# A Mamba scan on one core: weighted states added in pairs on VectorE, their sums transposed by TensorE, states ordered in pairs

## The reference

```
xb, z = split(x @ in_w.T)
xb = silu(causal_conv(xb, 4 taps) + cb)
delta, Bm, Cm = split(xb @ xp_w.T, [16, 16, 16])
delta = softplus(delta @ dtw.T + dtb)
dA = exp(delta[..., None] * -exp(a_log))
mi = delta[..., None] * Bm[:, :, None, :] * xb[..., None]
v = 0.6 * v + mi_t
h = dA_t * h + v
y_t = einsum("ben,bn->be", h, C_t)
y = (y + dp * xb) * silu(z)
out = y @ ow.T
```

## Time and profile before

| | us |
|---|---|
| median of 3 runs | 2259.93 (2258.51 to 2260.69) |
| profiled execution | 2258.78 |
| its span on the core | 2257.5 |
| TensorE busy | 1946.5 (86%) |
| TensorE weight loads | 1554.8 (69%) |
| VectorE busy | 1383.8 (61%) |
| GpSimd busy | 991.2 (44%) |
| ScalarE busy | 913.2 (40%) |

### The profile page before, as it was taken

The page is one execution under the profiler, slowest core; times in us unless marked ns, Lnnn a source line. Parts: engine busy times, 40 slices in busy tenths (PEclk is TensorE's granted clock), DMA queues, the critical chain, the costliest instruction groups (busy, mean ns, idle before and its releaser), DMA issues.

```text
span 2257.5 us, 31075 instructions
## 1 busy us (share of the span) xinstructions
PE 1946.5 (86%) x12488; PEld 1554.8 (69%) x12488; DVE 1383.8 (61%) x1752; ACT 913.2 (40%) x1302; POOL 991.2 (44%) x749
## 2 busy tenths in 40 slices
PE   4699999999999999999998676666856889999999
PEld 2578789788897888879996233322423378888888
DVE  3666777668577685777784544343633376666665
ACT  5555465464654646545441132233222521222221
POOL 1568679487695876958984110011012011112110
PEclk9889999999999999999999697978988989999999
DMA  4010001011010110102202520333033010001001
GB/s 154 1 39 28 30 20 39 19 39 38 20 38 19 39 38 20 39 19 76 88 26 59 126 59 19 83 75 75 1 75 76 1 57 19 19 20 38 1 1 38
DMA packets 30222, 94.43 MB, mean 42 GB/s; under 512 B 6912, under 2 KB 13440, under 8 KB 25600
## 3 DMA queue, kind: packets, MB, share of 16 engines
q1 hardware_dynamic: 25472, 79.85, 11.6%
q0 software_dynamic: 4608, 12.59, 2.5%
HBM read 56.24 MB, written 2.36 MB: 26 GB/s over the span
## 4 chain that ended last, share of the span: by engine, by line
PE 61%; DVE 12%; POOL 9%; issue 8%; SPq 5%; ACT 4%; DMA 2%; DVEq 0%; POOLq 0%; ACTq 0%
PE psum L416 15%; POOL hst L681 7%; PE psum L399 6%; PE psum L1225 5%; SPq L1140 5%; PE psum L1227 5%; PE psum L1226 5%; PE psum L355 5%; PE psum L898 3%; DVE nmax L1074 2%; PE psum L390 2%; DVE hst L516 2%; PE psum L928 2%; DVE hh L1375 2%; DVE uw L441 2%
## 5 line engine op out<-in xcount | busy, mean ns | idle before, releaser
L516 DVE TENSOR_TENSOR_SCAN hst<-dA,psum 128x512 f32<-128x512 f32 x512 | 616.8, 1215 | 296.3 <-PE psum L416 265.6
L681 POOL TENSOR_TENSOR hst<-hst,cb 128x512 f32<-128x512 f32 x512 | 662.2, 1313 | 279.3 <-DVE hst L516 278.0
L416 PEld LDWEIGHTS psum<-filt,c_early 128*128 128x128 f32 x2560 | 317.1, 195 | 57.3 <-issue 30.1
L416 PEld LDWEIGHTS psum<-filt,uT 128*128 128x128 f32 x2560 | 313.4, 193 | 48.2 <-issue 23.2
L416 PE MATMUL psum<-filt,c_early 128*128 128x112 f32 (+1 forms) x2560 | 321.9, 274 | 19.1 <-DVE hst L516 9.5
L416 PE MATMUL psum<-filt,uT 128*128 128x112 f32 (+1 forms) x2560 | 318.7, 272 | 19.2 <-DVE hst L516 9.8
L399 PE MATMUL psum<-ident,hst 128*128 128x128 f32 x2048 | 316.0, 278 | 12.7 <-POOL hst L681 12.0
L399 PEld LDWEIGHTS psum<-ident,hst 128*128 128x128 f32 x2048 | 246.4, 156 | 16.4 <-POOL hst L681 16.0
L993 ACT ACTIVATE pT<-psum 128x1024 f32<-128x1024 f32 x128 | 128.7, 1025 | 313.6 <-PE psum L938 312.8
L1147 POOL DMA_DIRECT2D qk<-parts x96 | 46.7, 495 | 461.0 <-PE psum L938 417.2
L619 ACT ACTIVATE dA<-delta,alog 128x512 f32<-128x512 f32 x256 | 181.2, 720 | 134.5 <-DVE hst L516 134.4
(11 more groups left out here) (176 smaller groups left out, 3159.9 us busy)
## 6 DMA issues: line engine op xcount, KB each, us to landing
cb<-c_rows SPq DMA_DIRECT2D x32, 1024.0 KB, 4.7
qk<-parts SPq DMA_DIRECT2D x160, 128.0 KB, 5.1
qk<-parts POOLq DMA_DIRECT2D x96, 128.0 KB, 6.1
raw<-up_dram SPq DMA_DIRECT2D x9, 512.0 KB, 3.9
raw<-down_dram SPq DMA_DIRECT2D x9, 512.0 KB, 4.8
xm<-x_dram SPq DMA_DIRECT2D x4, 512.0 KB, 10.6
w_early<-w_in_dram SPq DMA_DIRECT2D x2, 1024.0 KB, 9.9
c_early<-ctxT_dram SPq DMA_DIRECT2D x4, 512.0 KB, 5.5
```

The lines of the kernel that those rows point to most:

```text
L416: m = pe.matmul(bk[:, c * QC:c * QC + CH[c]], uT[k % 2][:, c, et * P:(et + 1) * P], filt[:, f % 2, c, n % GN, 0:CH[c]], start=True, stop=True)
L516: dve.tensor_tensor_scan(hst[:, i % NH, :], dA[:, i % NDA, :], bank("v", i), 0.0, ALU.mult, ALU.add).then_inc(scan_done, 1)
L681: pool.tensor_tensor(h, h, cb[:, q % 2, i // ET % GN, :], ALU.mult).then_inc(g_done, 1)
```

## The change

- TensorE no longer transposes every weighted state. VectorE adds the weighted state of the tile before to that of an odd tile, in place in `hst` (`dve_add_pair`), and TensorE transposes that sum alone (`pe_add_pair`).
- A pair must be two states of one block, so the order of tiles is another: two states of block 0, the same two of block 1, and so on (`tile_of`). The GpSimd rows of C, the filters and the decays follow this order; the groups of four states stay.
- VectorE adds the pair that ends PAIR_LAG = 3 tiles behind the scan just issued, right behind this scan and before its side steps; so an even scan is followed by an addition.
- LAG goes from 5 to 6 and `hst` from 6 to 8 buffers.
- The plan: the back's four blocks are two steps apart instead of one, and the front starts at step 9 instead of 6. With it conv begins at step 15 instead of 12, z at 20 (17), d at 32 (29), clip at 37 (34), max at 41 (38), u at 52 (48); the last c piece comes at 63 (60) together with its copy on ScalarE.

```diff
--- before.py
+++ after.py
@@ -161,8 +161,8 @@
             yT = xraw[:, :, NTAP - 1:]
             cb = sb(mc, "cb", [P, 2, GN, S])
             c_rows = nc.dram_tensor("c_rows", [NI, NSTATE, S], F32).ap()
-            NDA, AHEAD, LAG, NRING, Y0 = 5, 4, 5, 4, 4
-            NH = LAG + 1
+            NDA, AHEAD, PAIR_LAG, LAG, NRING, Y0 = 5, 4, 3, 6, 4, 4
+            NH = LAG + 2
             dA = sb(mc, "dA", [P, NDA, S])
             hst = sb(mc, "hst", [P, NH, S])
 
@@ -172,11 +172,16 @@
             zeroed, u_done, gated, filt_done = (sem(n) for n in ("zeroed", "u_done", "gated", "filt_done"))
             bank_full, v_full, y_full = sem("bank_full"), sem("v_full"), sem("y_full")
             bank_dve, bank_act = sem("bank_dve"), sem("bank_act")
-            c_stored, ld_c, g_done, y_out = sem("c_stored"), [sem("ld_c0"), sem("ld_c1")], sem("g_done"), sem("y_out")
+            c_stored, ld_c, g_done, y_out, pair_done = sem("c_stored"), [sem("ld_c0"), sem("ld_c1")], sem("g_done"), sem("y_out"), sem("pair_done")
             xs_done, conv_done, bend_done, clip_done, delta_done, rms_done, scan_done, alog_neg = (
                 sem(n) for n in ("xs_done", "conv_done", "bend_done", "clip_done", "delta_done", "rms_done", "scan_done", "alog_neg"))
             xbs_done, sz_done, exp_done, splus_done, sq_done, root_done, decay_done, alog_exp = (
                 sem(n) for n in ("xbs_done", "sz_done", "exp_done", "splus_done", "sq_done", "root_done", "decay_done", "alog_exp"))
+
+            def tile_of(i):
+
+                r = i % TILES
+                return i // TILES, 2 * (r // (2 * ET)) + r % 2, r // 2 % ET
 
             def rms_count(k):
                 return 1 if k == 0 else 2 if k < B else k - 1
@@ -252,7 +257,6 @@
                     s += 1
                     put("dve", "xd", e)
                     put("pool", "gate", e)
-                    s -= e < ET - 1
                 s += LAG + 1 if at != "last" else 1
                 for t in range(TB):
                     put("pe", "bo", t)
@@ -296,9 +300,9 @@
 
             plan_front(0, "first", 0)
             for k in range(NI):
-                s = LAG + 1
+                s = LAG + 3
                 if k:
-                    plan_back(k - 1, k, LAG - ET)
+                    plan_back(k - 1, k, LAG - 2 * ET + 2)
                 else:
                     s = plan_norms(k, ET)
                 if k + 1 < NI:
@@ -390,14 +394,14 @@
                         i = pe.matmul(bk[:, 0:D], sz[par][:, kt, j * P:(j + 1) * P], w_out[:, l, kt, :], start=kt == 0, stop=kt == ET - 1)
                 i.then_inc(bank_full, 1)
 
-            def pe_add_state(i):
-                k, n, et = i // TILES, i // ET % NSTATE, i % ET
-                pe.wait_ge(g_done, i + 1)
-                if k and n == 0:
+            def pe_add_pair(i):
+                k, n, et = tile_of(i)
+                pe.wait_ge(pair_done, i // 2 + 1)
+                if k and n == 1:
                     pe.wait_ge(y_out, ET * (k - 1) + et + 1)
                 for t in range(TB):
                     m = pe.matmul(psum[:, Y0 + et, t * P:(t + 1) * P], hst[:, i % NH, t * P:(t + 1) * P], ident[:],
-                                  start=n == 0 and t == 0, stop=n == NSTATE - 1, is_transpose=True, skip_group_check=True)
+                                  start=n == 1 and t == 0, stop=n == NSTATE - 1, is_transpose=True, skip_group_check=True)
                 if n == NSTATE - 1:
                     m.then_inc(y_full, 1)
 
@@ -416,12 +420,13 @@
                         m = pe.matmul(bk[:, c * QC:c * QC + CH[c]], uT[k % 2][:, c, et * P:(et + 1) * P],
                                       filt[:, f % 2, c, n % GN, 0:CH[c]], start=True, stop=True)
                     m.then_inc(v_full, 1)
-                    if i >= LAG:
-                        pe_add_state(i - LAG)
+                    if i >= LAG and (i - LAG) % 2:
+                        pe_add_pair(i - LAG)
                     for x in steps["pe"].get((k, i % TILES), []):
                         pe_side(*x)
                 for i in range(NI * TILES - LAG, NI * TILES):
-                    pe_add_state(i)
+                    if i % 2:
+                        pe_add_pair(i)
                 for x in at_steps("pe", "last"):
                     pe_side(*x)
 
@@ -496,6 +501,11 @@
                 dve.wait_ge(bank_dve, emptied_by("dve", NI - B + b, "bo", TB - 1))
                 dve.tensor_tensor(r, r, xm[:, toks(b), :], ALU.add).then_inc(x1_done, 1)
 
+            def dve_add_pair(i):
+                h = hst[:, i % NH, :]
+                dve.wait_ge(g_done, i + 1)
+                dve.tensor_tensor(h, h, hst[:, (i - 1) % NH, :], ALU.add).then_inc(pair_done, 1)
+
             def dve_mamba():
                 dve.memset(epst[:], EPS).then_inc(eps_set, 1)
                 dve.wait_ge(ld_x[0], 16)
@@ -514,8 +524,12 @@
                     if i % 2 == 0:
                         dve.wait_ge(decay_done, i + 2)
                     dve.tensor_tensor_scan(hst[:, i % NH, :], dA[:, i % NDA, :], bank("v", i), 0.0, ALU.mult, ALU.add).then_inc(scan_done, 1)
+                    if i >= PAIR_LAG and (i - PAIR_LAG) % 2:
+                        dve_add_pair(i - PAIR_LAG)
                     for x in steps["dve"].get((i // TILES, i % TILES), []):
                         dve_side(*x)
+                dve_add_pair(NI * TILES - 3)
+                dve_add_pair(NI * TILES - 1)
                 for x in at_steps("dve", "last"):
                     dve_side(*x)
                 dve_add_x(B - 1)
@@ -609,7 +623,7 @@
                     act_ln_root(LN2[0], 0, TB)
 
             def act_decay(a):
-                k, n, et = a // TILES, a // ET % NSTATE, a % ET
+                k, n, et = tile_of(a)
                 if a == 0:
                     act.wait_ge(alog_neg, 1)
                 if a % TILES == 0:
@@ -678,7 +692,7 @@
                         pool.wait_ge(ld_c[q % 2], 16 * (q // 2 + 1))
                     h = hst[:, i % NH, :]
                     pool.wait_ge(scan_done, i + 1)
-                    pool.tensor_tensor(h, h, cb[:, q % 2, i // ET % GN, :], ALU.mult).then_inc(g_done, 1)
+                    pool.tensor_tensor(h, h, cb[:, q % 2, tile_of(i)[1] % GN, :], ALU.mult).then_inc(g_done, 1)
                     for x in steps["pool"].get((i // TILES, i % TILES), []):
                         pool_side(*x)
                 for x in at_steps("pool", "last"):
```

## The result

The changed kernel takes 2345.14 us (median of 4 runs, 2342.63 to 2348.1) against 2259.22 of the kernel before, a ratio of 1.038 with an interval of 1.037 to 1.040: 86 us slower. I had forecast slower, by 16 us, in a range up to 2310. The direction held, the size did not.

What follows compares the result with a forecast made beforehand. TensorE was taken to set the beat, with GpSimd close behind. Items 1 to 6 +4, item 0 -3, last item +14 and tail +1 made +16 us: 2276 us as the median, range 2247 to 2310.

Steps and rivals of the forecast that it cites:

- first rival: All items: additions fall into GpSimd's gaps; stretches 27.4, 22, 27.5, 31.5, 26.5, some 9 us less an item: 2188 us; chance 0.20.
- its sum, 2276: Whole kernel: the stretches of an item, item 0, last item and tail added up, +16 us, 2276 us median; chance 0.60.
- The price for GpSimd: GpSimd's products beside additions: each addition holds GpSimd up by 0.45 us where it has a queue, bounds 0 and 0.67.
- TensorE's stretch, scans 19 to 31: Middle item, scans 19 to 31: TensorE binds, the stretch takes 27.5 us.
- scans 0 to 14: Middle item, first stretch: GpSimd binds, TensorE would need less, 30.8 us.
- the other signs: Changed profile: GpSimd nearly 90% busy, scans' longest wait not for TensorE, middle items 142 to 149 us.
- VectorE by itself would keep up with the 1.51 of today.: VectorE in the layers: 1.42 us a tile with additions, against TensorE's present 1.51 us a tile.
- the 2.84 of the prediction: VectorE, one pair of tiles: two scans of 1.13 us and an addition of 0.58 take 2.84 us.
- may carry 4 us over: Scans 32 to 47: GpSimd has 35.1 us of work, idles 4.1 and may carry 4 over, so 35.2 us.
- The second: Additions that meet a GpSimd queue: the whole addition blocks GpSimd, 0.22 us more each, +37, 2313 us; chance 0.10.
- The third: Additions at filters: a 3.94 us filter holds addition, scans and TensorE, which loses its clock; +41, 2317 us; chance 0.10.
- The last item: Item with no next front beside it: first half +5.5 us, second half +8.4, together +14.

Runs made afterwards that it cites:

- the maxima: Changed kernel with a one-input maximum along the 512 columns of the second state in each addition's place, filters in one block: 2274.8 us, 1.007.
- chunks: Each GpSimd filter cut into five pieces between products instead of one block: changed kernel 2296.1 us, with the maxima 2224.5, order and plan alone 2237.7, kernel before 2269.8.

## Why the prediction was wrong

By the runs, the 86 us are made of four terms, each the difference of two kernels, taken in this order. The forecast's terms follow from its first rival, 2188 us with no price on GpSimd, and its sum, 2276:

| part | forecast | measured |
|---|---|---|
| order, plan, lag, ring | 0 | +5 |
| half of the transposes gone | -72 | -48 |
| VectorE's time and place in the queue | 0 | +59 |
| exclusion of additions and GpSimd | +88 | +70 |
| in all | +16 | +86 |

So the price of exclusion was not too low in sum. The miss of 70 us is VectorE's 59 and 29 of transposes and order, less 18 of exclusion.

**What held.** GpSimd and VectorE exclude each other on such operations (the Trainium skill, SBUF — State Buffer, section Who interferes with whom; the products' median of 1630 against 1273 ns and the addition of 4.32 us beside a filter of 3.93 bear it out). The price for GpSimd was near: its products are busy for 763.8 us where I had named near 770, and in the quiet half a pair takes 3.03 us where my rates gave 2.92. TensorE's stretch, scans 19 to 31, was right, and so was the rest behind the layers. In scans 0 to 14 GpSimd is the busiest engine, 30.2 of 32.1 us, as I had it, but VectorE is close with 29.3. Of the other signs, GpSimd's share came to 77% and not to nearly 90, the scans' longest wait is still the one for TensorE, and items of 157 us are beyond the 150 that were named as the sign of additions that wait out whole filters, though with VectorE busy for 133 us and not throughout.

**The step that failed: "VectorE by itself would keep up with the 1.51 of today."** From it I charged nothing on VectorE's side. It compared rates, 1.42 us against 1.51, and already these were the wrong two: 1.51 is TensorE's beat with the transposes that the change removes. Timeline of VectorE in the quiet half without any addition, then with the maxima:

```profile
1144.39 2.34 DVE L526 TENSOR_TENSOR_SCAN hst<-dA,psum 128x512 f32<-128x512 f32 x2 [0.29 <-PE psum L420]
1147.01 2.34 DVE L526 TENSOR_TENSOR_SCAN hst<-dA,psum 128x512 f32<-128x512 f32 x2 [0.28 <-PE psum L420]
```

```profile
1194.25 0.66 DVE L507 TENSOR_REDUCE hst<-hst 128x1 f32<-128x512 f32 x1
1194.83 2.32 DVE L526 TENSOR_TENSOR_SCAN hst<-dA,psum 128x512 f32<-128x512 f32 x2
1197.06 0.66 DVE L507 TENSOR_REDUCE hst<-hst 128x1 f32<-128x512 f32 x1
```

A pair takes 2.62 us at TensorE's new beat and 2.81 with the maxima, where VectorE never idles; the 2.84 of the prediction was right, and above the new beat. And VectorE's queue is in order, and the change moves two more things into it. One is the wait of an addition for GpSimd: I had seen the 1.54 us row for L458, and priced only its counterpart on GpSimd. Measured, the additions wait 96 us. The other is that TensorE's transposes, which hung on GpSimd's product alone, now hang on VectorE's queue. Timeline at scan 42 of the same item:

```profile
808.21 0.87 DVE L507 TENSOR_TENSOR hst<-hst 128x512 f32<-128x512 f32 x1
...
813.79 0.18 DVE L468 RECIPROCAL stat<-stat 128x4 f32<-128x4 f32 x1 [3.58 <-ACT stat L545]
...
815.90 1.22 DVE L526 TENSOR_TENSOR_SCAN hst<-dA,psum 128x512 f32<-128x512 f32 x1 [1.34 <-ACT dA L633]
817.03 0.67 DVE L507 TENSOR_TENSOR hst<-hst 128x512 f32<-128x512 f32 x1
...
817.76 1.11 PE L403 MATMUL psum<-ident,hst 128*128 128x128 f32 x4 [5.79 <-DVE hst L507]
```

VectorE waits 3.58 us for ScalarE's root; the addition stands behind it, the front's max (L463) and a scan, and TensorE idles 5.79 us for that addition. Windows of 4 us there:

```profile
812.00:816.00 4.00, 0.00 (x0) 0.00 (x0) 0.86 (x3) 3.94 (x6) 0.00 (x0) 0.98 0.00 0
816.00:820.00 4.00, 2.24 (x11) 2.25 (x12) 4.00 (x4) 2.24 (x4) 2.80 (x2) 0.50 0.00 0
820.00:824.00 4.00, 4.00 (x25) 3.94 (x25) 4.00 (x5) 1.44 (x2) 3.92 (x4) 0.66 0.01 2
```

TensorE's clock is at 0.50, the lower of its two levels, behind the idle stretch and at 0.66 in the next one. The additions are not what brings this: over scans 43 to 47 the clock is 0.57 with order and plan alone, and 0.59 without any addition, where TensorE idles 4.5 us for a bank; in the kernel before, has 1.00 over scans 32 to 47. Windows of the kernel without additions, scans 36 to 42 and 43 to 47:

```profile
724.40:741.30 16.90, 12.43 (x112) 12.19 (x112) 10.54 (x11) 13.98 (x22) 9.52 (x8) 0.96 0.01 1
741.30:748.10 6.80, 6.80 (x39) 6.80 (x39) 6.80 (x8) 3.57 (x6) 6.80 (x5) 0.59 0.02 5
```

But they take 16.9 and 6.8 us there, 18.7 and 8.6 with the maxima, and 19.0 and 9.1 with the additions. So scans 32 to 47 take 40.4 us against 32.4 in the kernel without additions: 3.6 of the 8.0 for the addition at the filter (scans 32 to 35, 12.3 against 8.7), 3.5 for VectorE's time and place in the queue, as the maxima show it, and 0.9 for the exclusion in scans 36 to 47.

**A second step failed, in the sum: GpSimd "may carry 4 us over".** These 4 us were taken off scans 32 to 47 and charged nowhere. For scans 48 to 63 the prediction says that GpSimd "needs 19.8 + 3.9 + 3.6 = 27.3", though the earlier trace rows has it busy there for 28.27 us without any addition, which makes 31.9 with them. Measured, it is busy for 31.75 of the 32.9 us. Without any addition the stretch takes 31.7 us, where the first rival had 26.5, and that is the whole difference between this item (140.0 us) and the rival's stretches (134.9). Windows of scans 48 to 55 in that kernel; GpSimd is never idle:

```profile
748.10:764.60 16.50, 13.57 (x111) 13.30 (x110) 9.46 (x10) 8.61 (x13) 16.50 (x13) 0.90 0.17 64
```

So the removed transposes gave 48 us and not 72. With the maxima, chunks bring scans 48 to 63 to 27.9 us; no run has chunks with neither maximum nor addition and half of the transposes.

**The first rival** (TensorE's gain comes through) named the point from which it decides as a price of 0.39 us an addition on GpSimd. By the runs the balance of a pair is not there: transposes give 48 us, and VectorE's own share takes 59 even at no price on GpSimd, so that kernel is at 2274.8 us and not at 2188. **The second** (whole addition blocks GpSimd, products at 1.9 us) did not occur: the median is 1.63, and none of the 512 lasts between 1.8 and 2.0. **The third** put the filter's block in the right place, an addition that stands through a filter of 3.94 us and holds the scans and TensorE, but charged only the clock for it, 5 us an item. As a mechanism it was the nearest: 2317. It should have stood in the sum with the wait itself, up to 4 us at three filters an item, and not among the rivals at 0.10.

**The last item** was forecast at +14 and came to +2.7; 9.6 us of the difference lie in its first half. This hid 11 us of the error elsewhere.

## What to carry to other kernels

An engine's new rate has to be held against the other engines' beat after the change, not before it. An operation put into an in-order queue can cost more than its duration: its own waits hold everything behind it, and whoever now depends on it inherits every wait ahead of it; so list both before comparing rates. Where two engines exclude each other, price both sides of the meeting, and the longest operation of the other engine first. Work that a sum lets one stretch hand on has to turn up in the next one. A reading of an experiment's gain (here the chunks') needs the same edit on kernels without the suspected cause: it gained 26 and 50 us where VectorE had no addition, and lost 11 in the kernel before.

## What the runs showed of the hardware that I had not expected

A multiplication by a scalar on VectorE, fp32, SBUF to SBUF, took 392 ns for 511 columns in seven rows of 73, and it and GpSimd shut each other out: 20 of 256 lasted over 2.1 us, up to 4141 ns, and the products beside them had a median of 1364. A maximum along 512 columns took 653 to 686 ns with GpSimd at work all along and left its products at a median of 1.27 us. Cut into five, the filter of 3.93 us became pieces of 0.93 us in the median, 4.7 us a filter on average beside the maxima and 5.4 beside the additions.
